# The output bias of a masked attention: one product on TensorE, or one addition on GpSimd

## Reference

```python
def _L3_xattn_ref(query, key, value, mask, Wq, Wk, Wv, Wo, bo):
    Q = jnp.einsum('btd,ed->bte', query, Wq).reshape(B, Tq, H, -1).transpose(0, 2, 1, 3)
    K = jnp.einsum('btd,ed->bte', key, Wk).reshape(B, Tk, H, -1).transpose(0, 2, 1, 3)
    V = jnp.einsum('btd,ed->bte', value, Wv).reshape(B, Tk, H, -1).transpose(0, 2, 1, 3)
    scores = jnp.einsum('bhqd,bhkd->bhqk', Q, K) / jnp.sqrt(jnp.asarray(d_k, Q.dtype))
    scores = jnp.where(mask[:, None] == 0, jnp.asarray(-1000000000.0, scores.dtype), scores)
    attn = jax.nn.softmax(scores, axis=-1)
    Z = jnp.einsum('bhqk,bhkd->bhqd', attn, V)
    Zc = Z.transpose(0, 2, 1, 3).reshape(B, Tq, Dv)
    return jnp.einsum('btd,ed->bte', Zc, Wo) + bo

x = x + jnp.tanh(g_xattn[3]) * _L3_xattn_ref(_layernorm(x, axis=-1), ctx_1024, ctx_1024, mask_BxSxS2_if1, ...)
```

## Time and profile before

| | us |
|---|---|
| median of 3 runs | 1573.51 |
| the runs | 1571.66, 1573.51, 1576.69 |
| the profiled execution, its own time | 1574.3 |
| its span (first to last instruction) | 1572.5 |

### The profile page before, as it was taken

The page is one execution under the profiler, slowest core; times in us unless marked ns, Lnnn a source line. Parts: engine busy times, 40 slices in busy tenths (PEclk is TensorE's granted clock), DMA queues, the critical chain, the costliest instruction groups (busy, mean ns, idle before and its releaser), DMA issues. The chain is left out here.

```text
span 1572.5 us, 24867 instructions
## 1 busy us (share of the span) xinstructions
PE 1184.8 (75%) x8865; PEld 822.6 (52%) x8866; DVE 985.9 (63%) x1840; ACT 772.4 (49%) x1392; POOL 935.2 (59%) x1056
## 2 busy tenths in 40 slices
PE   4773569996369997426688868689997765899894
PEld 4432446654359995325455535446666444566563
DVE  5789869995531110434999869689991787444321
ACT  2487457775625443235577766457774431211220
POOL 4200149995245554642799878468884446478875
PEclk9796789998679998767799979879996896999997
DMA  2000011110238883110111000011100014244442
GB/s 105 8 0 0 1 33 34 34 34 5 60 117 242 235 226 102 39 32 14 49 34 34 18 16 1 17 34 34 34 18 2 26 38 161 63 97 81 98 89 23
DMA packets 61007, 89.89 MB, mean 57 GB/s; under 512 B 10251, under 2 KB 33430, under 8 KB 60502
## 3 DMA queue, kind: packets, MB, share of 16 engines
q1 hardware_dynamic: 45078, 70.07, 14.1%
q0 software_dynamic: 15808, 18.24, 6.8%
HBM read 56.96 MB, written 16.12 MB: 46 GB/s over the span
## 5 line engine op out<-in xcount | busy, mean ns | idle before, releaser
L1635 PE MATMUL ps<-topk_up_sb,topk_wu 128*128 128x512 f32 x256 | 122.6, 625 | 3.3 <-DVE sb_xnT L1755 2.6
L1536 ACT ACTIVATE topk_ga<-ps 128x512 f32<-128x512 f32 x64 | 38.2, 599 | 154.3 <-PE ps L1635 150.9
L205 POOL TENSOR_SCALAR sb_stage<-sb_x,l0f_rstd,l0f_shift 128x128 f32<-128x128 f32 x48 | 24.5, 525 | 146.1 <-DVE l0f_shift L192 145.9
L1459 POOL DMA_INDIRECT out<-topk_shared,l3f_route_slots x64 | 100.2, 1566 | 18.1 <-issue 18.0
L1755 DVE TENSOR_TENSOR sb_xnT<-topk_ga,ps 128x512 f32<-128x512 f32 x64 | 43.9, 688 | 102.3 <-ACT topk_ga L1536 97.8
L2114 DVE TENSOR_TENSOR l1f_g_y<-ps,l1f_g_wd 128x256 f32<-128x256 f32 x39 | 16.6, 425 | 136.9 <-PE ps L2057 121.2
L2084 ACT ACTIVATE l1f_g_h<-ps,l1f_g_wd 128x256 f32<-128x256 f32 x156 | 64.2, 474 | 72.7 <-DMA l1f_g_wd<-l1f_W 48.7
L1455 POOL DMA_INDIRECT topk_xg<-l3f_rows,l3f_route_slots x64 | 78.8, 1231 | 18.9 <-issue 18.4
L529 POOL TENSOR_TENSOR l3x_prob<-l3x_prob,l3x_rden 128x1232 f32<-128x1232 f32 x32 | 72.0, 2250 | 26.4 <-DVE l3x_rden L686 26.4
L1996 POOL DMA_INDIRECT l1f_g_xg<-l1f_rows,l1f_route_slots x78 | 75.1, 963 | 17.7 <-issue 12.8
L529 POOL TENSOR_TENSOR l1x_prob<-l1x_prob,l1x_rden 128x1232 f32<-128x1232 f32 x32 | 72.0, 2250 | 14.3 <-DVE l1x_rden L686 14.3
(11 more groups left out here) (510 smaller groups left out, 3565.0 us busy)
## 6 DMA issues: line engine op xcount, KB each, us to landing
l1f_g_wd<-l1f_W SPq DMA_DIRECT2D x39, 322.0 KB
l1f_g_wu<-l1f_W SPq DMA_DIRECT2D x39, 256.0 KB
topk_wu<-l3f_W SPq DMA_DIRECT2D x16, 512.0 KB
l1f_y_rows<-l1f_g_y SPq DMA_DIRECT2D x39, 128.0 KB
topk_wd<-l3f_W SPq DMA_DIRECT2D x16, 256.0 KB
l1x_vrows<-sb_l0f_up SPq DMA_DIRECT2D x16, 154.0 KB
l2x_vrows<-l2x_vall SPq DMA_DIRECT2D x16, 154.0 KB
l3x_vrows<-l3x_vall SPq DMA_DIRECT2D x16, 154.0 KB
```

The lines of the kernel that those rows point to most:

```text
L1459: pool.indirect_dma_start(out=out_rows, out_offset=spot(g, i), in_=y[g % 2][:, i, :], in_offset=None, compute_op=ALU.add).then_inc(y_added ...
L1635: ins = pe.matmul(ps[:, 2 * (c % 2) + i, :], wu[g % W][:, (i * CX + c) * P:(i * CX + c + 1) * P], xgT[g % 2][:], start=True, stop=True)
```

## The change

In the masked attention the output bias leaves TensorE. SP brings bo to all 128 partitions. GpSimd multiplies it once with the gate (gb), after its masks are made and ahead of its loop. In each iteration it adds gb to tile n of x (`bias`), behind add(n-1) and ahead of divide(n+2), and counts `biased`; add(n), one iteration later, waits for that count beside its wait for gated. TensorE's product of one row is left out there, and the output product opens and closes the accumulation by itself; its wait for the transfer goes too. The attention l1x keeps the product, which now reads the first row of a larger tile.

```diff
-        bo = sbs("bo", [1, D], 1)[0]
+        product_bias = bias_out and not masked
+        BP = P if masked else 1
+        bo, gb, gb_ready, biased = sbs("bo", [P, D], 1)[0], sbs("gb", [P, D], 1)[0], s.one("gb_ready"), s.one("biased")
...
             if bias_out:
-                sp.dma_start(bo[:], d[f"{layer}_bo"].partition_broadcast(1)).then_inc(loads, 16)
+                sp.dma_start(bo[0:BP, :], d[f"{layer}_bo"].partition_broadcast(BP)).then_inc(loads, 16)
...
+            def bias(n):
+                xb = t["x"][:, n * P:(n + 1) * P]
+                pool.tensor_tensor(xb, xb, gb[:], ALU.add).then_inc(biased, 1)
+
             def add(n):
                 pool.wait_ge(out_kept, n + 1)
+                if masked:
+                    pool.wait_ge(biased, n + 1)
                 xb = t["x"][:, n * P:(n + 1) * P]
                 pool.tensor_tensor(xb, xb, gated[n % 2][:], ALU.add).then_inc(residual, 1)
...
+            if masked:
+                pool.wait_ge(loads, 16)
+                pool.tensor_scalar(gb[:], bo[:], t["gate"][:, gate_at:gate_at + 1], None, ALU.mult).then_inc(gb_ready, 1)
+                pool.wait_ge(gb_ready, 1)
             for it in range(1 - AHEAD, NT):
...
                 if it >= 1:
                     add(it - 1)
+                if masked and it >= 0:
+                    bias(it)
                 if 0 <= it + AHEAD - 2 < NT:
                     divide(it + AHEAD - 2)
...
-                if bias_out:
-                    pe.matmul(OUT, t["ones"][0:1, :], bo[:], start=True, stop=False)
-                pe.matmul(OUT, oT[n % 2][:], w[:, 384:512], start=not bias_out, stop=True).then_inc(out_made, 1)
+                if product_bias:
+                    pe.matmul(OUT, t["ones"][0:1, :], bo[0:1, :], start=True, stop=False)
+                pe.matmul(OUT, oT[n % 2][:], w[:, 384:512], start=not product_bias, stop=True).then_inc(out_made, 1)
...
-            if bias_out:
+            if product_bias:
                 pe.wait_ge(loads, 16)
```

## The result

The change made the kernel faster, by more than I had forecast. The first comparison, four executions of each, gave 1555.89 us against 1575.10, a ratio of 0.988 (0.984 to 0.992). Repeated, six executions against 22: 1558.05 against 1570.99 us, 0.9903 (0.9879 to 0.9927). On a second chip, where both kernels are some 36 us shorter, 1521.86 against 1534.76 us, 0.9910 (0.9884 to 0.9936). The forecast was 8.2 us less, with a range down to 1562.0. The two repeats say 13 us less, and the first one 19 (17.6 against the median of 1573.51 us that stands ahead of the prediction). One more execution of the kernel before, of 2916.63 us, is in the slow state and left out.

What follows compares the result with a forecast made beforehand. TensorE was taken to bound the masked attention, VectorE close behind. At 4.65 us a turn, 6.5 + 1.1 - 0.2 + 0.8 = 8.2 us less: 1574.3 to 1566.1 (1565.3 for the median), range 1562.0 to 1571.5.

Steps and rivals of the forecast that it cites:

- The turn: One 128-row tile in the masked attention's middle: 4.89 us falls to 4.65, 0.24 less; 27 turns give 6.5 us.
- loop: TensorE and VectorE share one set of score banks: shift, mask, scores, maximum and shift again sum to 4.64 us a turn.
- the slack: Between GpSimd's add and VectorE's spread, which waits for it: 2.1 us; GpSimd falls behind by at most 0.3 in 27 turns.
- The end: Turns 28 to 31, without scores: 1.1 us gained, 0.2 taken back by division 31, 0.8 gained in the last turn.
- The start: Bias broadcast and gate multiplication ahead of GpSimd's loop: cost nothing, and would cost from 7 us of delay on.
- The new wait: GpSimd's add(n) waits for biased, fulfilled a whole turn earlier by the same engine: costed at nothing.
- Rivals 1: GpSimd's turn is 4.87 us by full durations, or 4.90; gain about 2.0, time 1571.5; chance 0.19 together with rival 2.
- 3: Rival: a VectorE reduction holds up GpSimd's bias, turn 5.37 us, 14.5 us more, 1588; chance 0.08.
- 2: Rival: mask product still starts about 0.4 us behind shift; only the end's 1.9 us stay, 1571.6; chance 0.19 with rival 1.
- Behind the stage stands a barrier, so the rest moves as a whole: After the masked attention, everything moves earlier by the stage's 8.2 us, with no gain or loss of its own.

Runs made afterwards that it cites:

- the cut kernel: The changed kernel cut to its last three stages, earlier results filled with constants, against the kernel before cut alike: medians 666.17 and 676.43 us.
- the two pauses: Useless GpSimd products ahead of the attention's last add: 1.3 us in the kernel before (ratio 0.9987), 1.7 us in the changed kernel (0.9952 of before).

## Why the prediction was wrong

By its own steps:

- **The turn: right.** 0.36 us off TensorE (weighing 1.52 us behind the transposes, with the same wait of 0.18 for ScalarE), 0.15 from shift to mask, 0.41 for the bias; loop 4.64 in the sum, 4.636 measured; GpSimd 4.65 in the sum, 4.66 measured. I charged the turn with GpSimd's 4.65. It went by the loop's 4.636, and GpSimd's lag of 0.02 a turn stayed in the slack. 27 turns gave 7.1 us instead of 6.5.
- **The end: right.** From the last row maximum to the last add 17.77 us became 16.06, 1.71 less; the sum had 1.1 - 0.2 + 0.8 = 1.7. Division 31 indeed followed its predecessor by 3.99 us (3.98 forecast).
- **The start: right.** Nothing was delayed.
- **The new wait: right.** It shows nowhere: the add with it takes 0.42 us by its starts.
- **Rivals 1 and 3, and 2: fell.** The bias costs 0.41 by its starts, no VectorE row grew (shift 1.43, maximum 1.44), and the mask product followed the shift after 0.15.
- **"Behind the stage stands a barrier, so the rest moves as a whole": the step that failed.** It gave the last stage zero. In three of four traces of the changed kernel that stage gained 4 us, since the shortened attention puts the clock's rise elsewhere against its work. The attention alone, 8.7 to 8.8 us in the two repeats, is inside the range; 8.7 and 4 make the measured 13. By the mean over the traces it would be 8.7 and 2.4, 11.1 us, which lies in the interval of the second repeat (9.8 to 17.8) and just below that of the first (11.5 to 19.0); so the 4 us are shown in the traces, and that they make up the whole rest of the medians is not. Taking the product away did not make the last stage faster by itself: with 1.7 us of idling the trace has the 4 us again.
- **The range was too narrow below for the same reason.** I used the scatter of three executions (5 us). 22 later ones of the kernel before span 1564.1 to 1579.2. The first comparison is a case of its own: its two traces both have the long stretch (102.4 and 102.5 us), so the 4 us are not in them. What they have beyond the forecast is 2.4 us in the stage, 2.2 ahead of it and 3.1 behind. Of the 2.4, the turns gave 0.6 and the clock most of the rest: the first score product ran at the upper clock (the first row maximum 2.3 us behind the stage's start, 3.4 before), which is 1.1 us, and the fourth turn gave another 0.7. The 2.2 ahead the next trace took back, and most of the 3.1 behind is open.

What stays open: why the last part of the last stage, behind the stretch, took 215.7 us in the first trace of before, and 208.7 to 214.8 in five others with times like that one's (203.5 to 207.2 on the two faster chips); it has no order by kernel. And the 19 us of the first comparison are more than 13 by an amount that only scatter explains so far.

The Trainium skill (TensorE: Matmul & The Clock Gate, Part 1) says that where TensorE's clock changes is not tied to the kernel's start, so the same kernel differs from run to run. The traces agree: the changed kernel showed 102.5 us once and 98.5 twice. They add that one version of this kernel met one case more often than the other version did (in five and six traces), so the effect need not average out of a comparison.

## What to carry to other kernels

Sum up the loops between engines, not only each engine's work: here the reader of a single set of score banks set the turn at 4.64 us, and that told beforehand that GpSimd's added 0.41 would be nearly free. On GpSimd, go by starts; the recorded durations would have said 4.87 and no gain. And where an edit shortens a stage ahead of a barrier, look at TensorE's granted clock in the first microseconds of the next stage, in more than one trace. A pause of a microsecond or two can help to tell the edit's own worth from the clock's, if its trace is read as well: of the two pauses here one did not move the rise to where it was meant to go.

## What the runs showed of the hardware

- Two GpSimd additions in place on one tile, the second waiting for the first, take 0.13 us more than two that do not wait (0.95 for the pair, 0.41 each). How much of it is the wait and how much the same tile was not told apart. A wait for one a turn old shows no cost.
- GpSimd's recorded spans can grow at unchanged distance of starts: a division reached 2.30 us in the first trace of the changed kernel against 2.25. It is not being busy alone that does it, for with the bias twice GpSimd has no idle time either and keeps 2.25.
- A row maximum that waits for the scores, even by a few hundredths, is recorded with 1.44 us and the next instruction starts 1.36 behind it; one that waits for nothing has 1.38 and 1.29.
- A pause of 1.7 us at the end of a stage with a barrier behind it cost 6.8 us by the medians (3.5 to 9.2 by my estimate).
- One of the 27 turns took 4.81 us instead of 4.63, the same one in all whole kernels that run at 4.64 us a turn. In it the row maximum starts 0.24 us behind the scores and not 0.07. It is absent in the cut kernel, and nothing here says what it is.
